# VectorE adds the last key block onto the running sum of exponentials, and the softmax sums take one matmul a head in place of two

## What is computed

```
q = (h @ Wq).reshape(b, s, 32, 32)
k, v = kv[..., :32], kv[..., 32:]
scores = einsum('bqhd,bkd->bhqk', q, k) * scale
scores = where(causal, scores + slopes * (key - query), -inf)
attn = softmax(scores, axis=-1)
out = einsum('bhqk,bkd->bqhd', attn, v).reshape(b, s, h)
x = x + out @ Wo
x = x + layernorm(x) @ dequantize(qweight).T + bias
```

## Time and profile before

| | us |
|---|---|
| median of 3 runs | 929.73 |
| lowest and highest of them | 925.4, 939.7 |
| the profiled execution's own time | 931.09 |
| its span, first to last instruction | 929.3 |
| PE busy | 872.2 (94%) |
| PEld busy | 628.3 (68%) |
| DVE busy | 542.0 (58%) |
| POOL busy | 397.0 (43%) |
| ACT busy | 335.4 (36%) |

### The profile page before, as it was taken

One profiled execution on the slowest core, in us unless ns is written; L12 is line 12 of the kernel. 1 busy time (PEld: TensorE's weight loads), 2 busy tenths in 40 slices (PEclk: granted clock), 3 DMA queues, 4 the chain that ended last, 5 costly groups with the idle time before them and its releaser, 6 DMA issues.

```text
span 929.3 us, 13775 instructions
## 1 busy us (share of the span) xinstructions
PE 872.2 (94%) x4912; PEld 628.3 (68%) x4912; DVE 542.0 (58%) x1469; ACT 335.4 (36%) x639; POOL 397.0 (43%) x254
## 2 busy tenths in 40 slices
PE   2799999999999999999999979969999999999996
PEld 2578888888855555555555545548888888888884
DVE  6454362532566787888788757126656455554553
ACT  2422222221066666667666636321211112211110
POOL 0000000000048778888888858626345433454211
PEclk9899999999979999999999979988999999999997
DMA  4544554648348754464454461175333553334111
GB/s 153 164 156 122 176 153 153 176 120 212 101 107 225 201 140 106 115 165 117 111 145 130 114 143 46 48 202 139 90 91 93 145 124 105 90 91 135 47 46 45
DMA packets 86892, 117.17 MB, mean 126 GB/s; under 512 B 8020, under 2 KB 50004, under 8 KB 86744
## 3 DMA queue, kind: packets, MB, share of 16 engines
q1 hardware_dynamic: 86824, 116.30, 46.2%
HBM read 76.95 MB, written 38.93 MB: 125 GB/s over the span
## 4 chain that ended last, share of the span: by engine, by line
PE 87%; DMA 5%; DVE 5%; ACT 1%; SPq 1%; issue 1%; POOL 0%; DVEq 0%; POOLq 0%; ACTq 0%
PE p_o L505 19%; PE p_st L668 14%; PE p_st L586 10%; PE p_s L654 10%; PE p_s L559 9%; PE p_o L597 9%; PE p_o L654 8%; PE p_o L610 4%; DMA xt<-ml 2%; PE p_st L505 2%; PE p_s L498 1%; DMA raw<-in_wq_dram 1%; DVE spill L920 1%; DMA inv_b<-inv_d 1%; PE p_st L576 1%
## 5 line engine op out<-in xcount | busy, mean ns | idle before, releaser
L920 DVE CUSTOM_DVE_ANT_0 spill<-p_s,mask 128x128 bf16<-128x128 f32 (+3 forms) x512 | 225.4, 486 | 82.3 <-PE p_s L559 80.6
L415 POOL TENSOR_SCALAR_AFFINE_SELECT pt<-pt 128x512 f32<-128x512 f32 x128 | 90.1, 716 | 317.2 <-ACT pt L761 317.2
L761 ACT ACTIVATE pt<-p_st 128x512 f32<-128x512 f32 (+1 forms) x352 | 181.4, 561 | 102.0 <-PE p_st L586 96.6
L505 PE MATMUL p_o<-xt,wqh 128*128 128x512 f32 x512 | 171.8, 402 | 3.7 <-DVE wql L1021 3.7
L559 PE MATMUL p_s<-kst,xt 98*128 98x128 f32 (+3 forms) x512 | 152.3, 336 | 6.5 <-DVE mx L920 6.5
L586 PE MATMUL p_st<-xt,kst 100*128 100x512 f32 (+1 forms) x352 | 148.5, 425 | 8.4 <-DMA xt<-ml 6.4
L505 PEld LDWEIGHTS p_o<-xt,wqh 128*128 128x128 f32 x512 | 98.3, 192 | 24.8 <-DVE wql L1021 4.1
L559 PEld LDWEIGHTS p_s<-kst,xt 98*128 98x128 f32 x512 | 101.0, 200 | 20.0 <-issue 9.7
L422 POOL TENSOR_TENSOR pt<-pt 128x1536 f32<-128x1536 f32 x32 | 111.7, 3490 | 2.7
L586 PEld LDWEIGHTS p_st<-xt,kst 100*128 100x128 f32 x352 | 68.3, 195 | 63.6 <-ACT pt L761 27.7
L505 PE MATMUL p_o<-xt,wql 128*128 128x512 f32 x256 | 101.5, 396 | 0.0
(11 more groups left out here) (102 smaller groups left out, 1201.5 us busy)
## 6 DMA issues: line engine op xcount, KB each, us to landing
xt<-qh_d SPq DMA_DIRECT2D x64, 256.0 KB
xin<-in_x_dram SPq DMA_DIRECT2D x16, 512.0 KB, 3.9
qh_d<-qh SPq DMA_DIRECT2D x32, 256.0 KB, 2.6
ql_d<-ql SPq DMA_DIRECT2D x32, 256.0 KB, 3.2
xt<-ql_d SPq DMA_DIRECT2D x32, 256.0 KB
o_d<-o_st SPq DMA_DIRECT2D x32, 256.0 KB, 2.5
ob<-o_d SPq DMA_DIRECT2D x16, 512.0 KB, 6.5
inv_b<-inv_d SPq DMA_DIRECT2D x64, 128.0 KB, 5.8
```

Source lines behind the costliest of these rows:

```text
L415: pool.affine_select(out=own, in_=own, compare_op=ALU.is_ge, fill=0.0, base=0, pattern=[[0, 4], [1, P]], channel_multiplier=-1).then_inc(c ...
L505: last = pe.matmul(dst, w[:, c, cols], xs[:, c, :], start=(c == 0 and k == 0), stop=(c == CK - 1 and k == 2))
L761: act.activation(pt[s % 2][:, j:j + heads, PT_AT[kb]:PT_AT[kb] + KB_LEN[kb]], p_st[:, place(k) % 3, 0:heads * KB_LEN[kb]].rearrange("p (j ...
L920: dve.tensor_tensor_reduce(spill[:, SPILL_AT[qb]:SPILL_AT[qb] + keys], scores_of(n), mask[:, S - keys:S], 1.0, LOWEST, ALU.add, ALU.max, m ...
```

## The change

Key block 3 (128 queries, four heads: 128x512 elements) is now added onto the sum by DVE, in a new function `add_last`. In step s it stands behind the eighth maximum, for step s - 1. It waits for both of POOL's additions and all cuts of that step. The last step's is run behind the loop. `totals` on PE has one part: four matmuls over 512 columns, which wait for DVE's new semaphore `last_added` in place of POOL's `add_done`.

```diff
-            def totals(s, part):
+            def totals(s):
                 b, g = s // GROUPS, s % GROUPS
-                if part == 0:
-                    at_least(pe, sums_taken, b if g == 0 else 0)
-                    pe.wait_ge(add_done, 2 * s + 2)
-                at, to = ((ADD_AT, slice(0, S)), (PT_AT[3], slice(2 * P, 3 * P)))[part]
+                at_least(pe, sums_taken, b if g == 0 else 0)
+                pe.wait_ge(last_added, s + 1)
                 for h in range(4):
-                    last = pe.matmul(p_sum[32 * h:32 * h + 32, to], pick[:, 7 - g:39 - g],
-                                     pt[s % 2][:, h, at:at + to.stop - to.start], start=(g == 0 and part == 0),
-                                     stop=(g == GROUPS - 1 and part == 1), tile_position=(0, 32 * h), skip_group_check=True)
-                if part == 1:
-                    last.then_inc(pv_done, 1)
+                    last = pe.matmul(p_sum[32 * h:32 * h + 32, :], pick[:, 7 - g:39 - g],
+                                     pt[s % 2][:, h, ADD_AT:ADD_AT + S], start=(g == 0),
+                                     stop=(g == GROUPS - 1), tile_position=(0, 32 * h), skip_group_check=True)
+                last.then_inc(pv_done, 1)
...
+            def add_last(s):
+                p = pt[s % 2]
+                dve.wait_ge(add_done, 2 * s + 2)
+                dve.wait_ge(cut_done, 4 * s + 4)
+                to = p[:, :, ADD_AT + 2 * P:ADD_AT + 3 * P]
+                dve.tensor_tensor(to, to, p[:, :, PT_AT[3]:PT_AT[3] + P], ALU.add).then_inc(last_added, 1)
...
                         maximum(first + i)
                     if i == 9 and s + 1 < STEPS:
                         max_low(s + 1)
+                    if i == 7 and s > 0:
+                        add_last(s - 1)
...
+            add_last(STEPS - 1)
             o_normal(1)
```

More of the change, by code:

```diff
@@ L188, in layer @@
             sem(n) for n in ("v_done", "pv_done", "o_taken", "sums_taken", "inv_done"))
+        last_added = sem("last_added")
         o_out, inv_out = sem("o_out"), sem("inv_out")
@@ L601, in values @@
                     last.then_inc(v_done, 1)
-            def totals(s, part):
+            def totals(s):
                 b, g = s // GROUPS, s % GROUPS
-                if part == 0:
-                    at_least(pe, sums_taken, b if g == 0 else 0)
-                    pe.wait_ge(add_done, 2 * s + 2)
-                at, to = ((ADD_AT, slice(0, S)), (PT_AT[3], slice(2 * P, 3 * P)))[part]
+                at_least(pe, sums_taken, b if g == 0 else 0)
+                pe.wait_ge(last_added, s + 1)
                 for h in range(4):
-                    last = pe.matmul(p_sum[32 * h:32 * h + 32, to], pick[:, 7 - g:39 - g],
-                                     pt[s % 2][:, h, at:at + to.stop - to.start], start=(g == 0 and part == 0),
-                                     stop=(g == GROUPS - 1 and part == 1), tile_position=(0, 32 * h), skip_group_check=True)
-                if part == 1:
-                    last.then_inc(pv_done, 1)
+                    last = pe.matmul(p_sum[32 * h:32 * h + 32, :], pick[:, 7 - g:39 - g],
+                                     pt[s % 2][:, h, ADD_AT:ADD_AT + S], start=(g == 0),
+                                     stop=(g == GROUPS - 1), tile_position=(0, 32 * h), skip_group_check=True)
+                last.then_inc(pv_done, 1)
             VALUES_AT = {1: (0,), 4: (1,), 6: (2, 3)}
-            TOTALS_AT = {9: (0, 1)}
+            TOTALS_AT = 9
             FIRST_AT = {4: 0, 6: 1, 8: 2, 10: 3}
@@ L634, in attend @@
                             values(s - 1, kb)
-                        for part in TOTALS_AT.get(at, ()):
-                            totals(s - 1, part)
+                        if at == TOTALS_AT:
+                            totals(s - 1)
                     if s == STEPS - 1 and at in FIRST_AT:
@@ L692, in _ @@
                 out_proj(0, 4 + kb)
-            for part in range(2):
-                totals(STEPS - 1, part)
+            totals(STEPS - 1)
             for t in range(-1, TILES):
```

## The result

The changed kernel takes 952.20 us in the median (950.89 to 952.62, 4 runs) against 929.48 before (4 runs). The ratio is 1.0237, with a 95% interval of 1.0188 to 1.0286: slower, clear of the noise; whether by more or less than 2% the interval leaves open. Its profiled execution took 952.38 of its own, with a span of 950.0.

The account below looks back on a forecast made before the run. PE, and equally the chain through `ml`, bounded the turn. Added turn costs, less 0.2 after the loop, gave 24.8 us: 955.9 against the profiled 931.09, or 955 as a median (929.7 + 24.8 = 954.5); range 941 to 968.

Parts of the forecast that it names:

- The chain through `ml`: Attention turn: PE's weight load starts at 459.28, just after DVE's `ml` ends at 459.22, so this bounds the 9.73 us turn equally.
- The loop through POOL: Turn would close through PE's weight load, exponential, POOL's masking and additions (ending 8.79 later), new addition, two maxima, `ml`.
- PE's saving: Dropping four narrow matmuls a step shortens PE's work by 0.23 us each, 7.4 over 32 steps, 12.9 at most.
- `wo_low` turns: Eight attention turns of about 10.8 us with DVE's `wo_low` addition; each forecast 0.89 longer, 7.1 together.
- The addition's length: DVE's new 128x512 float32 addition, taken as 0.68 us from an existing 512-element row with one input in PSUM.
- Who goes first: After POOL's second addition, POOL's next cut was forecast to run before DVE's addition and hold it off; chance 0.58.
- its nearest row: Profile rows L990 on DVE and L438 on POOL, both begun at 634.54: POOL ended undisturbed, DVE 1.08 us later.
- The rival that DVE goes first: DVE's addition takes the shared port lock before POOL's cut: 0.64 us more a turn, 946 in all; chance 0.22.
- The 13 plain turns: Attention turns of 9.71 to 9.75 us without `wo_low` or late transfers; each forecast 0.98 longer.
- The four turns in which PE came late: Turns delayed by the transfer of `ml` or the last steps' order; forecast 0.4 us more each, 1.5 together.
- three near-plain ones: Attention turns of 9.93 to 10.02 us, whose late DMA is swallowed in part; forecast 0.7 more each.
- Behind the attention: After the loop, the last step's addition is done before PE needs it, so PE saves 0.2 us.

## Why the prediction was right

955 was forecast and 952.2 measured; the sum of the steps was +24.8 us, and the profiled executions lie 21.3 apart. The mechanism is the one forecast. That the total came so near is in part luck: single terms missed by up to 2.8 us, in both directions, as listed here.

- **What bounds the kernel.** Right. The chain through `ml` was taken for as tight as PE itself, from an ending 0.06 ahead. The run with `ml` ahead of the addition shows it: with `ml` on time the loss is gone. PE's wait for `ml` in a plain turn is 1.10, where about 1.2 was expected.
- **The loop through POOL.** Right. POOL's end stayed 8.78 behind place 8, and PE's saving was spent in it: the run that kept the narrow matmuls took the same time, with the same 10.7 turns.
- **PE's saving.** 0.23 a turn was taken over the 0.40 of busy time. Measured 0.20 a plain turn with the narrow ones left out, and none in the `wo_low` turns.
- **The addition's length.** 0.68 was taken, 0.69 measured alone.
- **Who goes first.** POOL, as its nearest row had it. The addition is 1.10 long in most plain turns (forecast: about 1.1). The cut's row begins 0.07 to 0.11 ahead of it there, so POOL was first by that much, and it was no tie. The rival that DVE goes first needed 0.7. Making POOL wait gave back 0.42 of each plain turn; that rival's sum had 0.34 less in each.
- **The turns.** 10.71 was forecast, 10.68 to 10.74 measured; behind a `wo_low` step 10.41 to 10.44. With `wo_low` +0.89 was forecast and +0.97 measured in the mean (7.7 for 7.1). The 13 plain turns gave 11.3 for 12.7, since four of them are the first or follow a `wo_low` step (0.37 to 0.70 longer each, not 0.98).
- **The four turns in which PE came late.** The forecast was +1.5; they came out 1.1 shorter in total, while one of the three near-plain ones grew by 1.96, to 11.94 (those three: 3.4 for 2.1). The first transpose is 1.4 later for 0.6, the last turn 0.97 longer for 1.0. PE's waits for the transfer of `ml` moved: one of 0.97 came one step earlier, one of 0.71 is gone, and the longest fell from 4.74 to 3.16. These terms were mis-sized, by the arrival of a few transfers.
- **Behind the attention.** 0.2 less was forecast, 3.0 less measured (from the last transpose to the end 351.16 for 354.15). The windows over it, with the stretch's length first, PE's busy time next and the granted clock third from the end, are

```profile
575.15:929.30 354.15, 335.94 (x1558) 264.54 (x1554) 175.03 (x185) 69.05 (x120) 141.00 (x59) 0.97 0.37 99
```

for the kernel before and

```profile
598.84:950.00 351.16, 332.45 (x1534) 261.09 (x1530) 174.17 (x188) 69.33 (x120) 139.99 (x59) 0.98 0.37 100
```

for the changed one. The clock was granted at 0.97 and 0.98 of 2.4 GHz, and PE was busy for 3.5 us less. A clock higher by 0.01 would make 336 us of busy time shorter by about 3.4 (an estimate from these rows). So the 3.0 isn't put down to the change.
- **The clock in the longer turns.** It was not expected to fall with a pause of a microsecond a turn, and didn't: over 255 to 598.84 the granted clock is 0.98, with 0.97 before (255 to 575.15). In windows of 10 us it is 1.00 in all of them from 275 to 565 in the changed kernel. It is lower only near the two ends of the stage, where PE stops for longer, and so it is in the kernel before (0.61 in 545 to 555, behind a pause of 4.74). The rule that was weighed there is that pauses which return in each loop bring PE back to its lower clock (the Trainium skill, TensorE: Matmul & The Clock Gate, "HAM oscillation — how this bites in real kernels"). This trace shows no sign of it at pauses of 1.1 us.

The one thing that the forecast left out is that its own reading pointed to a better place. The addition was priced where it stood; two maxima further down, behind `ml`, it costs nothing, and the change as a whole then comes out at 0.999 and 0.994 of the kernel before.

## What to carry to other kernels

An instruction in an in-order queue costs what stands behind it. Before adding one, look for the next instruction of that queue for which another engine already waits with no margin, and put the new one behind that. Where the new instruction waits for a third engine, write down the loop that this closes: if it no longer passes through the engine that was to be relieved, that engine's saving is worth nothing. And where a VectorE instruction reads two tensors from SBUF, look at what GpSimd runs at that moment: here even a masking with one input in SBUF, begun 0.08 earlier, held it off to its end.

## What the runs showed of the hardware

- A VectorE addition of 128x512 in float32, both inputs and the output in SBUF, takes 0.69 us alone, and 0.67 right behind another instruction.
- Released by the end of a GpSimd instruction, with the next GpSimd instruction queued right behind that, VectorE's addition began 0.07 to 0.11 behind the latter in all 19 such steps of the changed kernel, and was held off: 1.10 in place of 0.69, ending 0.53 to 0.55 behind the cut's end. The GpSimd instruction (a masking with one input and 0.65 long) was not slowed.
- Begun 0.32 behind the cut's start, in the middle of it, the addition was held off for 0.19 only (0.88), and again ended 0.55 behind the cut's end (the run with `ml` first). So the holding off lasted until the running GpSimd instruction ended.
